# Two transposed operands made by VectorE from block-exchanged loads, in place of TensorE transposes and ScalarE copies

## The chip, the cores and the metric

The kernel runs on one core of a Trainium2 chip. The metric is the device time of one launch in microseconds (us). A launch works through 64 batch items in one program; all operands are f32. The engines are TensorE (PE; its weight loads are listed as PEld), VectorE (DVE), ScalarE (ACT), GpSimd (POOL) and SyncE (SP), which issues most DMAs.

## What is computed

For each item, x is 128 nodes by 128 features and adj a symmetric-patterned but not symmetric 128 x 128 weight matrix. Two graph layers follow each other:

```python
hi = x @ W1[:H];  hj = x @ W1[H:]
h  = relu(hi[:, None, :] + hj[None, :, :] + b1)      # all 128 x 128 pairs of nodes
y  = layernorm(h @ W2 + b2) * gamma + beta
x  = layernorm(x + einsum('ij,ijh->ih', adj, y))
# second layer
Wh = x @ W_w.T + W_b;  s = si[:, None] + sj[None, :] + a_b
e  = exp(s) * adj;     x = layernorm(x + (e / e.sum(1)) @ x)
```

Nearly all the work is the pair product: 16384 rows of 128 features per item, through the 128 x 128 matrix W2.

## The kernel before

**The slot.** One item's pair work is one slot of the program, run by every engine in its own order (`run_slots`, L152 to L161): six slots are written out, a loop with a body of eight slots turns seven times, and the last four are written out again. Within a slot there are 16 units (`u`) of eight nodes i each; a unit is two quarters (`k`) of four nodes. In slot t the engines work on three items at once: the pairs of item t (`pairs`), the weighted sum over the pairs of item t-1 (`gather`), the rest of both layers for item t-2 (`tail`), and they prepare item t+1 (`prep`). The parity p picks one of two buffers.

**The pair pipeline.** GpSimd writes the sums hi + hj of a unit into `h` (L260, a ring of four units), ScalarE applies relu in place two units ahead (L289), TensorE multiplies by `w_pair` into one of four PSUM buffers `y_ps` (L611, each product done by the helper `mm` at L535 as four column groups of 32), ScalarE copies each quarter to `y` in SBUF (L397 calls `copy`, L271), and VectorE forms the sum of squares of each row from the PSUM and the SBUF copy (L521), which frees the PSUM buffer. TensorE waits for that at L609: quarter k needs the squares of quarter k-4. The weighted sums of the item before (`weighted_sums`, L580) stand behind units 4, 6, 7, 9, 10, 12, 13 and 15 (`SUM_AT`).

**The preparation of item t+1.** SP loads x and adj two items ahead into `x_in` and `adj_in` (L185, L187), each once TensorE has read the buffer's last contents (`xT_ps_s`, `adjT_ps_s`). TensorE, ahead of unit 5, multiplies each by the identity into two quarters of the PSUM tensor `prep_ps` (`prep_transposes`, L538 to L545). ScalarE copies them to `xT` and `adjT` in unit 7 (`prep_copies`, L273, and the call at L342). TensorE, ahead of unit 9, multiplies xT by the two halves of W1 (`prep_products`, L547). VectorE moves the products to `aT` and `bT` ahead of the squares of unit 9 (`project`, L379), and GpSimd's sums read these. `adjT` is read by GpSimd at L234 and L236, as weights for the sum over the pairs.

**Other loads.** SP also loads x and adj of item t-1 a second time, as rows (`x_res`, `adj_res`, L192, L193; two semaphores, used by VectorE in unit 1 and GpSimd in unit 6 of the next slot), and stores the output (L197) when VectorE has written it in unit 14.

**The set-up** (L386 to L428 on VectorE, L554 to L573 on TensorE) builds constants and folded weights, and prepares item 0 in the same way. ScalarE's queue issues nine small loads of weights, the last of them `beta_rows`.

Each engine's order of work is written out by hand at fixed places (unit u, and on VectorE the pair e of the unit's four pairs of squares); no scheduler moves anything.

Of the kernel before, what the change touches and what calls it, by code (L numbers as in the profile page):

```python
# [33 lines left out]
def gnn_pair_kernel(nc, x, adj, W1, b1, W2, b2, gamma, beta, Ww, Wb, aw, ab, out):  # L34
# [14 lines left out]
    GROUPS, GROUP = 4, 32  # L49
# [13 lines left out]
    with ctx:  # L63
# [6 lines left out]
        def sem(name):  # L70
            return ctx.enter_context(nc.semaphore(name))
# [28 lines left out]
        xT = sb("xT", [H, S])  # L100
# [33 lines left out]
        s_two, s_zero, s_part = sem("twos_preset"), sem("wz_zeroed"), sem("parts_marked")  # L134
        x_loaded, adj_loaded, xres_loaded, stored = (
            [sem(f"{n}_{p}") for p in range(2)] for n in ("x_loaded", "adj_loaded", "xres_loaded", "out_stored"))
        xT_ps_s, adjT_ps_s, adjT_sb_s = sem("xT_in_psum"), sem("adjT_in_psum"), sem("adjT_in_sbuf")
        ab_ps_s, ab_sb_s = sem("ab_in_psum"), sem("ab_in_sbuf")
        u_ready, h_ready = sem("preact_ready"), sem("h_ready")
        y_in_psum, y_stored, q_done = sem("y_in_psum"), sem("y_stored"), sem("q_done")  # L140
# [29 lines left out]
        @block.sync  # L170
        def _(sp):

            for b in range(2):
                sp.dma_start(x_in[:, b, :], x[b]).then_inc(x_loaded[b], 16)
                sp.dma_start(adj_in[:, b, :], adj[b]).then_inc(adj_loaded[b], 16)
                if b == 0:
                    sp.dma_start(w1a[:], W1[0:H, :]).then_inc(s_w1, 16)
                    sp.dma_start(w1b[:], W1[H:2 * H, :]).then_inc(s_w1, 16)
                    sp.dma_start(b1c[:], b1.rearrange("(p o) -> p o", o=1)).then_inc(s_w1, 16)

            def slot(t, half, p, pairs, prep, gather, tail, early):
                if pairs and not (isinstance(t, int) and t + 2 >= B):

                    sp.wait_ge(xT_ps_s, t + 1)
                    sp.dma_start(x_in[:, p, :], x[bass.ds(t + 2, 1)].rearrange("o s h -> (o s) h")).then_inc(x_loaded[p], 16)  # L185
                    sp.wait_ge(adjT_ps_s, t + 1)
                    sp.dma_start(adj_in[:, p, :], adj[bass.ds(t + 2, 1)].rearrange("o s h -> (o s) h")).then_inc(adj_loaded[p], 16)  # L187
                if gather:
                    if early >= 3:

                        sp.wait_ge(x_beta_ready, t - 2)
                    sp.dma_start(x_res[:, 1 - p, :], x[bass.ds(t - 1, 1)].rearrange("o s h -> (o s) h")).then_inc(xres_loaded[1 - p], 16)  # L192
                    sp.dma_start(adj_res[:, 1 - p, :], adj[bass.ds(t - 1, 1)].rearrange("o s h -> (o s) h")).then_inc(xres_loaded[1 - p], 16)  # L193
                if tail:

                    sp.wait_ge(out_ready, t - 1)
                    sp.dma_start(out[bass.ds(t - 2, 1)].rearrange("o s h -> (o s) h"), x_out[:]).then_inc(stored[p], 16)  # L197

            run_slots(sp, slot)

            for p in range(2):
                sp.wait_ge(stored[p], 16 * (B // 2))
# [66 lines left out]
        def _(act):  # L269
            def copy(dst, src):  # L270
                return nc.scalar.activation(dst, src, ACT.Copy)  # L271

            def prep_copies(b, early):  # L273


                act.wait_ge(adjT_ps_s, b + 1)
                if early >= 1:

                    act.wait_ge(ab_ps_s, b)
                copy(xT[:], prep_ps[:, 0, :])  # L280
                if early >= 2:

                    act.wait_ge(w_ready, b - 1)
                    act.wait_ge(adjS_ready, b - 1)

            def relu(t, u):

                act.wait_ge(u_ready, t * UNITS + u + 1)
# [10 lines left out]
            act.dma_start(abc[:], ab.broadcast_to([S, 1])).then_inc(s_w, 16)  # L299
            act.dma_start(beta_rows[:], beta.rearrange("(o k) -> o k", o=1).broadcast_to([S, K])).then_inc(s_w, 16)  # L300
            nc.scalar.preload_act_table_set("natural_log_exp_and_others")
            prep_copies(0, 0)
            copy(adjT[:, 0, :], prep_ps[:, 1, :]).then_inc(adjT_sb_s, 1)
            for u in range(2):
                relu(0, u)

            def slot(t, half, p, pairs, prep, gather, tail, early):
                for u in range(UNITS):
# [27 lines left out]
                    if tail and u == 7:  # L336
# [2 lines left out]
                        nc.scalar.activation(ln1[:], mv1[:, 1:2], ACT.Ln, bias=epsc[:, 0:1]).then_inc(ln1_ready, 1)  # L339
                        act.wait_ge(ln1_ready, t - 1)  # L340
                        nc.scalar.activation(rs1[:], ln1[:], ACT.Exp, scale=-0.5).then_inc(rs1_ready, 1)  # L341
                    if prep and u == 7:  # L342
                        prep_copies(t + 1, early + 1)
                        copy(adjT[:, 1 - p, :], prep_ps[:, 1, :]).then_inc(adjT_sb_s, 1)
                    if tail and u == 9:
                        act.wait_ge(si_ready, t - 1)
                        act.wait_ge(sj_ready, t - 1)
# [28 lines left out]

        @block.vector
        def _(dve):
            def project(b, p):  # L379

                dve.wait_ge(ab_ps_s, b + 1)
                nc.vector.tensor_copy(aT[:, p, :], prep_ps[:, 2, :])
                nc.vector.tensor_scalar(bT[:, p, :], prep_ps[:, 3, :], b1c[:, 0:1], None, ALU.add).then_inc(ab_sb_s, 1)


            for p in range(2):  # L386
                nc.vector.memset(y[:, p, :, LAST:S], 2.0).then_inc(s_two, 1)
            nc.vector.memset(x1e[:], 1.0).then_inc(s_setup_dve, 1)

            dve.wait_ge(s_const, 6)  # L390
            nc.vector.reduce_sum(part[:], ident[:].rearrange("p (c s) -> p s c", s=CHUNK), axis=mybir.AxisListType.X).then_inc(s_part, 1)
# [36 lines left out]
            def slot(t, half, p, pairs, prep, gather, tail, early):  # L428

                for u, e in ((u, e) for u in range(UNITS) for e in range(2 * QPU)):  # L430
# [46 lines left out]
                    if tail and (u, e) == (7, 2):  # L477
                        nc.vector.tensor_tensor_reduce(out=s_terms[:, 0, :], in0=x1p, in1=v2row[:], scale=rs1[:, 0:1], scalar=score_c[:, 0:1],
                                                       op0=ALU.mult, op1=ALU.add, accum_out=s_ij[:, 1:2]).then_inc(sj_ready, 1)
                    if prep and (u, e) == (9, 0):  # L480
                        if early >= 1:

                            dve.wait_ge(u_ready, t * UNITS)
                        project(t + 1, 1 - p)
# [46 lines left out]
        def _(pe):  # L531
            def mm(dst, lhsT, rhs):
                for g in range(GROUPS):
                    cols = slice(g * GROUP, (g + 1) * GROUP)
                    last = nc.tensor.matmul(dst[cols], lhsT[:, cols], rhs, start=True, stop=True, tile_position=(0, g * GROUP))  # L535
                return last

            def prep_transposes(b, p, loads, later):  # L538
                pe.wait_ge(x_loaded[p], loads)
                if later:  # L540

                    pe.wait_ge(ab_sb_s, b)
                mm(prep_ps[:, 0, :], x_in[:, p, :], ident[:]).then_inc(xT_ps_s, 1)
                pe.wait_ge(adj_loaded[p], loads)
                mm(prep_ps[:, 1, :], adj_in[:, p, :], ident[:]).then_inc(adjT_ps_s, 1)  # L545

            def prep_products(b):  # L547

                pe.wait_ge(adjT_sb_s, b + 1)
                mm(prep_ps[:, 2, :], w1a[:], xT[:])  # L550
                mm(prep_ps[:, 3, :], w1b[:], xT[:]).then_inc(ab_ps_s, 1)


            pe.wait_ge(s_const, 6)  # L554
            prep_transposes(0, 0, 16, False)

            pe.wait_ge(s_w, 16 * 9)
            pe.wait_ge(s_setup_dve, 8)
# [3 lines left out]
            mm(tail_ps[:, 2, :], a2rep[:], ww[:]).then_inc(s_setup_pe, 1)  # L562
            mm(tail_ps[:, 3, 0:1], wbrep[:], a12[:]).then_inc(s_setup_pe, 1)
            pe.wait_ge(s_w1, 16 * 3)
            prep_products(0)

            pe.wait_ge(s_setup_dve, 14)
            mm(att_ps[:, 1:2], b2c_rep[:], b2c[:]).then_inc(s_setup_pe, 1)
# [15 lines left out]
            def slot(t, half, p, pairs, prep, gather, tail, early):  # L584
                for u in range(UNITS):
                    if tail and u == 3:
                        pe.wait_ge(o_stored, t - 1)
                        if gather:

                            pe.wait_ge(ln_v_ready, t)  # L590
                        mm(tail_ps[:, 0, :], o_sb[:], ident[:]).then_inc(oT_ps_s, 1)
                    if tail and u == 5:
                        pe.wait_ge(oT_sb_s, t - 1)
                        mm(tail_ps[:, 1, :], oT_sb[:], w_back[:]).then_inc(f_ps_s, 1)
                    if prep and u == 5:
                        prep_transposes(t + 1, 1 - p, nth16(half, p, 1), True)
                    if prep and u == 9:
                        prep_products(t + 1)
                    if tail and u == 11:
                        pe.wait_ge(x1s_ready, t - 1)  # L600
                        pe.wait_ge(adjS_ready, t - 1)
                        mm(att_ps[:, 0:K + 1], adjS[:, p, :], x1s[:]).then_inc(att_done, 1)
                    if pairs:

                        pe.wait_ge(h_ready, t * UNITS + u + 1)
                        for k in range(u * QPU, (u + 1) * QPU):
                            if not (early == 0 and k < YRING):

                                pe.wait_ge(q_done, t * QUARTS + k - YRING + 1)  # L609
                            for n in range(QUART):  # L610
                                last = mm(y_ps[k % YRING][:, n, :], h[:, u % HRING, (k % QPU) * QUART + n, :], w_pair[:])  # L611
                            last.then_inc(y_in_psum, 1)
                    if gather and u in SUM_AT:
                        if SUM_AT[u] == 0:

                            pe.wait_ge(w_ready, t)
                            if early >= 2:
                                pe.wait_ge(o_stored, t - 1)
                        weighted_sums(1 - p, SUM_AT[u])
# [27 lines left out]
```

## Time and profile before

| what | value |
|---|---|
| median of 3 runs | 2435.99 us (2434.59 to 2438.61) |
| the profiled execution's own time | 2439.17 us |
| its span | 2437.4 us |
| mean granted TensorE clock | 0.996 |
| busy: TensorE, weight loads, VectorE, ScalarE, GpSimd | 98%, 84%, 87%, 91%, 83% |
| DMA queue q1 | 46512 packets, 21.12 MB, 3.1% of 16 engines |

The span is from the first to the last instruction in the trace; the time of a run has some 2 us around it. Busy time of TensorE is modelled and pipelined, so that a busy engine is not one at its peak, and the durations of overlapping matmuls add up to more than the time they take. Times of single instructions in the rows below are microseconds from the start of the span unless they are marked ns. The chain of waits follows the work that ended last back from the end, at each step to what released it or to the instruction before it on the same engine.

### The profile page before, as it was taken

What the parts mean: (1) busy time and instruction counts of PE and PEld (TensorE: products, weight loads), DVE (VectorE), ACT (ScalarE), POOL (GpSimd) and SP (SyncE); (2) the same over time, 40 slices, a digit from 0 to 9 for tenths busy, and PEclk for the clock granted to TensorE, in tenths of its full rate; (3) what the DMA queues carried; (4) which work ended last, traced back from release to release, by engine and by line L of the source; (5) the groups of instructions that cost most, each with busy time, mean ns of one, the idle gap of its engine ahead of it and who ended that gap; (6) DMA issues with size and microseconds to landing.
All of it is one profiled execution on the core that took longest, in us unless ns stands there. A gap on an engine that the chain in (4) does not pass through costs nothing.

```text
span 2437.4 us, 180631 instructions
## 1 busy us (share of the span) xinstructions
PE 2377.7 (98%) x73280; PEld 2049.3 (84%) x73280; DVE 2119.3 (87%) x17881; ACT 2221.6 (91%) x3841; POOL 2021.5 (83%) x1227
## 2 busy tenths in 40 slices
PE   8999999999999999999999999999999999999997
PEld 7888888888888888888888888888788888888885
DVE  7888888888888888988888888888888988889887
ACT  7999999989999999998999989999899998999996
POOL 8888888888888888888888888888788887888884
PEclk9999999999999999999999999999999999999999
DMA  0000000000000000000000000000000000000000
GB/s 20 10 14 15 10 16 16 10 17 13 13 16 10 17 16 10 16 15 13 16 10 16 16 11 16 10 16 16 11 15 13 12 16 11 16 16 10 16 10 10
DMA packets 48682, 33.37 MB, mean 14 GB/s; under 512 B 6208, under 2 KB 47808, under 8 KB 47808
## 3 DMA queue, kind: packets, MB, share of 16 engines
q1 hardware_dynamic: 46512, 21.12, 3.1%
q8 instruction: 596, 9.76, 1.7%
q14 instruction: 278, 2.28, 0.3%
q10 hardware_dynamic: 1296, 0.20, 0.1%
HBM read 17.11 MB, written 4.19 MB: 9 GB/s over the span
## 4 chain that ended last, share of the span: by engine, by line
PE 80%; ACT 10%; issue 5%; DVE 3%; POOL 2%; ACTq 0%; DMA 0%; POOLq 0%; DVEq 0%
PE y_ps L535 59%; PE agg_ps L580 17%; ACT h L289 5%; ACT y L271 3%; PE prep_ps L535 2%; DVE squares L521 2%; POOL h L260 2%; ACT beta_part L329 1%; PE tail_ps L535 1%; ACT ln_v L318 1%; PE att_ps L535 1%; DVE q L521 0%; ACT rstd L323 0%; ACTq L370 0%; DMA beta_rows<-in_L_gnn_beta_dram 0%
## 5 line engine op out<-in xcount | busy, mean ns | idle before, releaser
L260 POOL TENSOR_TENSOR h<-bT,aT 128x1024 f32<-128x1024 f32 x1024 | 1949.6, 1918 | 360.8 <-PE y_ps L535 338.2
L535 PEld LDWEIGHTS y_ps<-w_pair,h 128*32 128x32 f32 x65536 | 1834.9, 110 | 288.2 <-issue 213.3
L521 DVE CUSTOM_DVE_ANT_0 squares<-y_ps,y 128x128 bf16<-128x128 f32 x8192 | 1853.7, 285 | 247.2 <-ACT y L271 236.6
L535 PE MATMUL y_ps<-w_pair,h 128*32 128x128 f32 x65536 | 1964.0, 273 | 38.4 <-issue 21.0
L271 ACT ACTIVATE y<-y_ps 128x508 f32<-128x508 f32 x2048 | 1153.1, 595 | 159.6 <-PE y_ps L535 153.1
L289 ACT ACTIVATE h<-h 128x1024 f32<-128x1024 f32 x1024 | 1085.0, 1060 | 23.8 <-POOL h L260 20.5
L521 DVE DVE_READ_ACCUMULATOR2_ANT q<- 128x1 f32 x8192 | 679.4, 83 | 0.2
L580 PE MATMUL agg_ps<-y,wz 128*32 128x512 f32 x4096 | 548.3, 594 | 0.0
L580 PEld LDWEIGHTS agg_ps<-y,wz 128*32 128x32 f32 x4096 | 137.1, 110 | 4.0 <-issue 3.8
L454 DVE SCALAR_TENSOR_TENSOR o_sb<-agg_ps,part,o_sb 128x128 f32<-128x128 f32 x192 | 66.5, 346 | 0.2
L234 POOL TENSOR_TENSOR wz<-adjT,rstd 128x128 f32<-128x128 f32 x64 | 33.6, 525 | 33.9 <-ACT rstd L323 33.9
L535 PEld LDWEIGHTS att_ps<-x1s,adjS 128*32 128x32 f32 x512 | 20.2, 110 | 37.6 <-issue 32.7
L513 DVE TENSOR_SCALAR x_out<-att_ps,mv,rs 128x128 f32<-128x128 f32 x64 | 26.2, 410 | 28.7 <-ACT rs L360 28.7
L535 PEld LDWEIGHTS tail_ps<-w_back,oT_sb 128*32 128x32 f32 x512 | 18.2, 111 | 37.2 <-issue 36.1
L246 POOL TENSOR_TENSOR x_beta<-beta_part,x_res 128x128 f32<-128x128 f32 x64 | 29.6, 462 | 11.2 <-ACT beta_part L329 11.2
L436 DVE TENSOR_SCALAR tail_ps<-q,bnorm 128x128 f32<-128x128 f32 x64 | 22.6, 354 | 14.5 <-issue 12.3
L472 DVE TENSOR_SCALAR x1e<-att_ps,mv,rs 128x128 f32<-128x128 f32 x64 | 26.2, 410 | 8.5 <-ACT rs L341 4.7
L535 PE MATMUL att_ps<-x1s,adjS 128*32 128x129 f32 x512 | 28.1, 275 | 3.5 <-ACT x1s L354 3.5
L535 PE MATMUL tail_ps<-ident,o_sb 128*32 128x128 f32 x512 | 26.4, 273 | 4.3 <-DVE o_sb L454 4.3
L535 PE MATMUL prep_ps<-ident,x_in 128*32 128x128 f32 x512 | 26.8, 275 | 3.1 <-DMA x_in<-in_x_dram 3.1
L329 ACT ACTIVATE beta_part<-beta_rows,adj_sum 128x128 f32<-128x128 f32 x64 | 25.5, 398 | 3.0 <-DVE adj_sum L442 3.0
L535 PE MATMUL prep_ps<-xT,w1b 128*32 128x128 f32 x512 | 28.0, 275 | 0.0
(89 smaller groups left out, 679.7 us busy)
## 6 DMA issues: line engine op xcount, KB each, us to landing
x_in<-in_x_dram SPq DMA_DIRECT2D x64, 64.0 KB, 2.5
adj_in<-in_adj_dram SPq DMA_DIRECT2D x64, 64.0 KB, 2.2
x_res<-in_x_dram SPq DMA_DIRECT2D x64, 64.0 KB, 2.0
adj_res<-in_adj_dram SPq DMA_DIRECT2D x64, 64.0 KB, 2.0
out_dram<-x_out SPq DMA_DIRECT2D x64, 64.0 KB, 1.8
w<-in_L_gnn_W_dram ACTq DMA_DIRECT2D x1, 64.0 KB, 2.3
w1a<-in_L_gnn_W_dram SPq DMA_DIRECT2D x1, 64.0 KB, 2.2
w1b<-in_L_gnn_W_dram SPq DMA_DIRECT2D x1, 64.0 KB, 2.4
```

What stands on the lines that cost most here:

```text
L234: nc.gpsimd.tensor_tensor(columns, adjT[:, 1 - p, :].rearrange("j (g c s) -> j g c s", g=GROUPS, s=CHUNK), rstd[:].rearrange("j (c s g) -> ...
L246: nc.gpsimd.tensor_tensor(x_beta[:], beta_part[:], x_res[:, p, :], ALU.add).then_inc(x_beta_ready, 1)
L260: nc.gpsimd.tensor_tensor(h[:, u % HRING].rearrange("k (r g) s -> k r g s", g=GROUPS), bT[:, p, :].unsqueeze(1).unsqueeze(1).broadcast_to( ...
L271: return nc.scalar.activation(dst, src, ACT.Copy)
L289: nc.scalar.activation(h[:, u % HRING], h[:, u % HRING], ACT.Relu).then_inc(h_ready, 1)
L329: nc.scalar.activation(beta_part[:], beta_rows[:], ACT.Identity, scale=adj_sum[:, 0:1]).then_inc(beta_part_ready, 1)
L454: nc.vector.scalar_tensor_tensor(out=o_sb[:], in0=agg_ps[:, e * K:(e + 1) * K], scalar=part[:, e:e + 1], in1=o_sb[:], op0=ALU.mult, op1=AL ...
L472: nc.vector.tensor_scalar(x1e[:, 0:K], x1p, mv1[:, 0:1], rs1[:, 0:1], ALU.subtract, ALU.mult).then_inc(x1_ready, 1)
L513: nc.vector.tensor_scalar(x_out[:], x2p, mv2[:, 0:1], rs2[:, 0:1], ALU.subtract, ALU.mult).then_inc(out_ready, 1)
L521: last = nc.vector.tensor_tensor_reduce(out=squares[:, k % YRING, n, :], in0=y_ps[k % YRING][:, n, :], in1=y[:, p, i, :], scale=1.0, scala ...
L535: last = nc.tensor.matmul(dst[cols], lhsT[:, cols], rhs, start=True, stop=True, tile_position=(0, g * GROUP))
L580: last = nc.tensor.matmul(agg_ps[g * GROUP:(g + 1) * GROUP, :], wz[:, g, chunk, :], y_chunk[:, :, g, :], start=(chunk == 0), stop=(chunk = ...
```

## The change

x and adj of an item are loaded by four DMAs each instead of one (`load_blocks`): block n of 32 partitions gets, from each block m of 32 rows, the columns of block n. So the sixteen 32 x 32 blocks arrive exchanged across the diagonal, each of them untransposed, and each contiguous run is 128 bytes. VectorE's transpose then turns each 32 x 32 block in place on its way from `x_in` to `xT` and from `adj_in` to `adjT`, ahead of the first and the third pair of squares of unit 6. The TensorE products with the identity and the two ScalarE copies go. SP's wait before the next load is for VectorE's transpose, and TensorE's products wait for xT alone. The waits that protected xT and adjT from being overwritten move from ScalarE to VectorE. In the set-up VectorE transposes item 0 before it builds its constants.

```diff
@@ SP
+            def load_blocks(dst, src, sem):
+
+                for n in range(GROUPS):
+                    rows = slice(n * GROUP, (n + 1) * GROUP)
+                    sp.dma_start(dst[rows].rearrange("r (m c) -> r m c", c=GROUP),
+                                 src[:, rows].rearrange("(m r) c -> r m c", r=GROUP)).then_inc(sem, 16)
             for b in range(2):
-                sp.dma_start(x_in[:, b, :], x[b]).then_inc(x_loaded[b], 16)
-                sp.dma_start(adj_in[:, b, :], adj[b]).then_inc(adj_loaded[b], 16)
+                load_blocks(x_in[:, b, :], x[b], x_loaded[b])
+                load_blocks(adj_in[:, b, :], adj[b], adj_loaded[b])
...
-                    sp.wait_ge(xT_ps_s, t + 1)
-                    sp.dma_start(x_in[:, p, :], x[bass.ds(t + 2, 1)].rearrange("o s h -> (o s) h")).then_inc(x_loaded[p], 16)
-                    sp.wait_ge(adjT_ps_s, t + 1)
-                    sp.dma_start(adj_in[:, p, :], adj[bass.ds(t + 2, 1)].rearrange("o s h -> (o s) h")).then_inc(adj_loaded[p], 16)
+                    sp.wait_ge(xT_sb_s, t + 1)
+                    load_blocks(x_in[:, p, :], x[bass.ds(t + 2, 1)].rearrange("o s h -> (o s) h"), x_loaded[p])
+                    sp.wait_ge(adjT_sb_s, t + 1)
+                    load_blocks(adj_in[:, p, :], adj[bass.ds(t + 2, 1)].rearrange("o s h -> (o s) h"), adj_loaded[p])
@@ ScalarE
-            def prep_copies(b, early):
-                act.wait_ge(adjT_ps_s, b + 1)
...
-                copy(xT[:], prep_ps[:, 0, :])
...
-                    if prep and u == 7:
-                        prep_copies(t + 1, early + 1)
-                        copy(adjT[:, 1 - p, :], prep_ps[:, 1, :]).then_inc(adjT_sb_s, 1)
@@ VectorE
+            def transpose_x(b, p, loads, later):
+
+                dve.wait_ge(x_loaded[p], loads)
+                if later:
+
+                    dve.wait_ge(ab_ps_s, b)
+                nc.vector.transpose(xT[:], x_in[:, p, :]).then_inc(xT_sb_s, 1)
+
+            def transpose_adj(b, p, loads, later):
+
+                dve.wait_ge(adj_loaded[p], loads)
+                if later:
+
+                    dve.wait_ge(w_ready, b - 1)
+                    dve.wait_ge(adjS_ready, b - 1)
+                nc.vector.transpose(adjT[:, p, :], adj_in[:, p, :]).then_inc(adjT_sb_s, 1)
...
             nc.vector.memset(x1e[:], 1.0).then_inc(s_setup_dve, 1)
+            transpose_x(0, 0, 16 * GROUPS, False)
+            transpose_adj(0, 0, 16 * GROUPS, False)
...
+                    if prep and (u, e) == (6, 0):
+                        transpose_x(t + 1, 1 - p, nth16(half, p, 1) * GROUPS, True)
+                    if prep and (u, e) == (6, 2):
+                        transpose_adj(t + 1, 1 - p, nth16(half, p, 1) * GROUPS, early >= 1)
@@ TensorE
-            def prep_transposes(b, p, loads, later):
-                pe.wait_ge(x_loaded[p], loads)
...
-                mm(prep_ps[:, 0, :], x_in[:, p, :], ident[:]).then_inc(xT_ps_s, 1)
-                pe.wait_ge(adj_loaded[p], loads)
-                mm(prep_ps[:, 1, :], adj_in[:, p, :], ident[:]).then_inc(adjT_ps_s, 1)
-            def prep_products(b):
-                pe.wait_ge(adjT_sb_s, b + 1)
+            def prep_products(b, later):
+                pe.wait_ge(xT_sb_s, b + 1)
+                if later:
+                    pe.wait_ge(ab_sb_s, b)
                 mm(prep_ps[:, 2, :], w1a[:], xT[:])
                 mm(prep_ps[:, 3, :], w1b[:], xT[:]).then_inc(ab_ps_s, 1)
...
-                    if prep and u == 5:
-                        prep_transposes(t + 1, 1 - p, nth16(half, p, 1), True)
                     if prep and u == 9:
-                        prep_products(t + 1)
+                        prep_products(t + 1, True)
```

## Rows read from the trace of the kernel before

**Rows 1.** The page: span, busy time by engine, and the chain by engine.
```profile
PE 2377.7 (98%) x73280; PEld 2049.3 (84%) x73280; DVE 2119.3 (87%) x17881; ACT 2221.6 (91%) x3841; POOL 2021.5 (83%) x1227
PE 80%; ACT 10%; issue 5%; DVE 3%; POOL 2%; ACTq 0%; DMA 0%; POOLq 0%; DVEq 0%
```

**Rows 2.** The chain of waits through one slot: start, length, what.
```profile
1213.20 0.04 ACT y L271
...
1219.05 1.95 PE y_ps L535 x64
...
1222.08 0.44 PE prep_ps L535 x16
1222.52 3.49 PE y_ps L535 x128
1226.01 0.86 PE agg_ps L580 x8
...
1250.21 0.04 ACT y L271
```

**Rows 3.** Groups of instructions: adj_in times identity; count, busy us, mean ns.
```profile
L535 PE MATMUL prep_ps<-ident,adj_in 128*32 128x128 f32 x512 | 26.8, 275 | 0.0
```

**Rows 4.** TensorE's timeline from the transposes (unit 5) to unit 8.
```profile
1221.90 0.40 PE L535 MATMUL prep_ps<-ident,x_in 128*32 128x128 f32 x8
...
1222.34 3.68 PE L535 MATMUL y_ps<-w_pair,h 128*32 128x128 f32 x128
...
1229.29 1.93 PE L535 MATMUL y_ps<-w_pair,h 128*32 128x128 f32 x64
```

**Rows 5.** ScalarE's timeline: relu of unit 7, the copy of xT, y copies of units 7 and 8.
```profile
1222.43 1.06 ACT L289 ACTIVATE h<-h 128x1024 f32<-128x1024 f32 x1
...
1228.14 0.28 ACT L271 ACTIVATE xT<-prep_ps 128x128 f32<-128x128 f32 x1
...
1228.47 1.09 ACT L271 ACTIVATE y<-y_ps 128x508 f32<-128x508 f32 x2
...
1231.29 0.60 ACT L271 ACTIVATE y<-y_ps 128x508 f32<-128x508 f32 x1 [0.28 <-PE y_ps L535]
```

**Rows 6.** Groups of instructions: VectorE's sum over adj_res.
```profile
L442 DVE TENSOR_REDUCE adj_sum<-adj_res 128x1 f32<-128x128 f32 x64 | 18.0, 281 | 0.0
```

**Rows 7.** The timeline of the set-up: GpSimd's first sums and VectorE's vmean.
```profile
12.41 7.52 POOL L260 TENSOR_TENSOR h<-bT,aT 128x1024 f32<-128x1024 f32 x4 [10.36 <-DVE bT L383]
12.69 1.66 DVE L415 TENSOR_SCALAR vmean<-vsum 128x2 f32<-128x2 f32 x1
```

**Rows 8.** VectorE's timeline: end of unit 5's squares, starts of units 6 and 7.
```profile
1226.04 0.08 DVE L521 DVE_READ_ACCUMULATOR2_ANT q<- 128x1 f32 x1
1226.39 0.29 DVE L521 CUSTOM_DVE_ANT_0 squares<-y_ps,y 128x128 bf16<-128x128 f32 x1 [0.26 <-ACT y L271]
...
1229.10 0.29 DVE L521 CUSTOM_DVE_ANT_0 squares<-y_ps,y 128x128 bf16<-128x128 f32 x1 [0.46 <-ACT y L271]
```

**Rows 9.** GpSimd's timeline: h of units 6 to 10.
```profile
1218.56 9.61 POOL L260 TENSOR_TENSOR h<-bT,aT 128x1024 f32<-128x1024 f32 x5
```

**Rows 10.** SP's timeline: the last two loads of a slot.
```profile
1247.44 0.38 SPq L192 DMA_DIRECT2D x_res<-in_x_dram  x1
1247.91 0.38 SPq L193 DMA_DIRECT2D adj_res<-in_adj_dram  x1
```

**Rows 11.** The page: the DMA queue of SP; a load's KB and us to landing.
```profile
q1 hardware_dynamic: 46512, 21.12, 3.1%
...
x_in<-in_x_dram SPq DMA_DIRECT2D x64, 64.0 KB, 2.5
```

**Rows 12.** The timeline of the set-up: first load, gdiag, the products of item 0.
```profile
0.75 0.39 SPq L174 DMA_DIRECT2D x_in<-in_x_dram  x1
...
7.99 0.28 DVE L395 TENSOR_SCALAR gdiag<-ident,gcol 128x128 f32<-128x128 f32 x1 [5.19 <-DMA beta_rows<-in_L_gnn_beta_dram]
...
10.56 0.66 PE L535 MATMUL prep_ps<-xT,w1a 128*32 128x128 f32 x8
```

More of the change, by code:

```diff
@@ L136, in gnn_pair_kernel @@
             [sem(f"{n}_{p}") for p in range(2)] for n in ("x_loaded", "adj_loaded", "xres_loaded", "out_stored"))
-        xT_ps_s, adjT_ps_s, adjT_sb_s = sem("xT_in_psum"), sem("adjT_in_psum"), sem("adjT_in_sbuf")
+        xT_sb_s, adjT_sb_s = sem("xT_in_sbuf"), sem("adjT_in_sbuf")
         ab_ps_s, ab_sb_s = sem("ab_in_psum"), sem("ab_in_sbuf")
@@ L271, in copy @@
                 return nc.scalar.activation(dst, src, ACT.Copy)
-            def prep_copies(b, early):
-                act.wait_ge(adjT_ps_s, b + 1)
-                if early >= 1:
-                    act.wait_ge(ab_ps_s, b)
-                copy(xT[:], prep_ps[:, 0, :])
-                if early >= 2:
-                    act.wait_ge(w_ready, b - 1)
-                    act.wait_ge(adjS_ready, b - 1)
             def relu(t, u):
@@ L301, in _ @@
             nc.scalar.preload_act_table_set("natural_log_exp_and_others")
-            prep_copies(0, 0)
-            copy(adjT[:, 0, :], prep_ps[:, 1, :]).then_inc(adjT_sb_s, 1)
             for u in range(2):
@@ L554, in _ @@
             pe.wait_ge(s_const, 6)
-            prep_transposes(0, 0, 16, False)
             pe.wait_ge(s_w, 16 * 9)
@@ L564, in _ @@
             pe.wait_ge(s_w1, 16 * 3)
-            prep_products(0)
+            prep_products(0, False)
             pe.wait_ge(s_setup_dve, 14)
```

## The prediction, as it was put on record

> **What bounds the kernel now.** First the page's busy shares and its chain of waits [rows 1]: TensorE is busy 98% of the span and carries 80% of the chain, ScalarE 10%. The busy share alone would not settle it, so I followed the chain through one slot in order of time [rows 2]. A slot is one batch item; 37.0 us of chain lie between 1213.20 and 1250.21. It has two stretches. From 1213.2 to 1219.05, the head of the slot, the chain runs through ScalarE's copies and relus and then VectorE's squares, because TensorE has nothing else between its first four units and waits for a free PSUM buffer. From 1219.05 to 1250.19, 31.1 of 37 us, the chain is TensorE and nothing else: each piece starts where the last one ends. The two transposes (16 matmul records, 0.44 us at 1222.08) lie inside that second stretch, back to back with the pair products of unit 5 behind them. The whole question is therefore whether 0.44 us taken out there stays out.
>
> **What it removes.** TensorE: eight records for x and eight for adj per item, 512 of adj over the run [rows 3] and as many of x. Their busy time and their 275 ns apiece overlap, so the price is the chain's 0.44 us per item [rows 2]. Slots 0 to 62 prepare an item (63 of them); the 64th pair of transposes is in the set-up. 63 x 0.437 = 27.5 us (0.437 is 1221.90 to 1222.34 on the matmuls' own timeline [rows 4], which is the chain's 0.44). The weight loads lie beside them and go with them. ScalarE: the copies of xT and adjT stand between 1228.14 and the next y copy at 1228.47, so they take 0.33 us of its time [rows 5]. At that place ScalarE isn't on the chain, and 3 us later, in unit 8, it waits 0.28 us for TensorE [rows 5], so I count this at nothing; it would be a gain only if ScalarE were the late one there.
>
> **What it adds on VectorE.** Two 32x32-block transposes per item, ahead of the first and third pair of squares of unit 6. No such operation stands in the trace. Nearest from below: VectorE's sum of adj_res, also 128 elements per partition of f32 from SBUF, 281 ns [rows 6]. Zero is the lower end, since they could fit into idle time. Nearest from above: vmean, 1.66 us for two elements, of which more under the rivals [rows 7]. I take 0.3 us each, next to the like-sized row, 0.6 us together if nothing overlaps. [...]
>
> Is it? The ring has four PSUM buffers, and a unit fills two, so TensorE's unit 8 needs the squares of unit 6. VectorE is through with unit 5 at 1226.04 plus the accumulator read, idles 0.26 us for ScalarE, and starts unit 6 at 1226.39; eight squares at 0.21 us end at 1228.1 [rows 8]. With 0.6 us on top, and the idle time not counted, that is 1228.7. TensorE starts unit 8 at 1229.29 [rows 4], and with the change at 1228.85, its second quarter 0.87 us later at 1229.7. The first quarter of unit 6 would be done by 1227.6, the second by 1228.7: 1.2 and 1.0 us to spare. Unit 7 has the x1 and score steps on VectorE, and an idle time of 0.46 us before its squares [rows 8] takes up most of what the transposes shift; TensorE meanwhile has the sum of unit 9 and both products ahead of what needs them. The cover is VectorE's roughly 1 us of lead over the ring; if it is gone, each further 0.1 us costs 6 us over the run.
>
> What follows the removed matmuls must also keep up. Units 5 and 6 start 0.44 us earlier, at 1221.9 instead of 1222.34 [rows 4]. GpSimd is then writing h without a pause from 1218.56 to 1228.17, five units at 1.92 us [rows 9], and is the engine I looked at longest: those are h of units 6 to 10, and unit 7 isn't needed before 1226.2, when its h has been ready since 1222.4 and its relu since 1223.5 [rows 5]. No loss there. At the end of the slot all engines wait for TensorE again, so the next head starts in the same state, and its stall (16 units at 1.745, 8 sums at 0.86 and 7 small products at 0.22 are 36.3 us of work [rows 2], so 0.7 us per slot) stays as it was. I count no gain and no loss for it.
>
> **What moves on the queues.** The loads become eight DMAs of 16 KB in place of two of 64 KB, in 128-byte runs. SP issues its DMAs in one burst ahead of each slot, 0.47 us apart [rows 10]; six more are 2.8 us of SP. Behind them stand x_res and adj_res, not needed before unit 1 of the next slot, over 35 us later, and behind those the wait for the output, which comes 30 us later. x and adj themselves are asked for about two units before a slot and read in unit 6 of the slot after it. The new waits on SP (xT and adjT in SBUF) were met in unit 6 of the slot before. The hardware queue q1 holds 46512 packets and 3.1% of 16 engines' time [rows 11]: 1209 us of engine time, 26 ns a packet. The change adds 64 x 2 x 384 = 49152 packets; at the same 26 ns, the upper end, that is 80 us more for each of 16 engines over the run, 3.3% of the span. Lower end: nothing, since the bytes stay the same. Hidden either way, with 50 us between the issue and the use. The added wait on VectorE for loads that landed long ago holds up nothing.
>
> **The start.** VectorE now waits for x and adj before the constants part, centre and basis. SP issues every 0.47 us from 0.75, so the eighth load goes out at 4.0 and lands by 6.5 (2.5 us to landing [rows 11]); two transposes and 0.7 us of constants end near 7.9. The next step, gdiag, starts at 7.99 when beta_rows has landed [rows 12]. w1a, w1b and b1c go out six issues later, b1c at about 5.4, and land at 8.2; TensorE wants them at 10.56 [rows 12]. So 0 to 1 us, and I take 0.5.
>
> **The sum.** 27.5 - 0.5 = 27.0 us off. The profiled execution took 2439.2 us with a span of 2437.4, which makes 2412.2 for it; the median of the three runs is 2436.0, 3.2 below, and from it the forecast is **2409 us**, 1.1% faster. A measurement of this kernel can tell about 0.2%, 5 us, from no change.
>
> **Rival 1: the shared memory port (slower).** In the set-up vmean, a VectorE operation on two elements from SBUF to SBUF, starts at 12.69, 0.28 us into GpSimd's first h, and ends at 14.35, just as that h (1.9 us) does [rows 7]. It was shut out by GpSimd. None of VectorE's operations in the steady part suffers this, but nearly all have an operand in PSUM; the transposes have not. If they are shut out likewise, each waits up to 1.92 us, since GpSimd runs without a gap just there [rows 9], and 0.96 in the mean. Against 1.0 us of lead plus 0.44 gained, it decides from 1.44 us of waiting per slot on: two mean waits (1.92) make 0.5 us per slot lost, 30 us, 2467; two full ones 2.4 us, 2587. Against it: adj_sum reads and writes SBUF alone too, also with GpSimd working, and takes 281 ns in the mean of 64 [rows 6]. [...] Chance 0.12.
>
> **Rival 2: the gain is partly given back.** Units 5 and 6 run without a sum between them, and ScalarE goes from y copy to relu almost without a gap after the head. If TensorE, 0.44 us earlier, meets a ring that ScalarE or VectorE hasn't emptied, or six more DMAs in SP's burst delay something behind them, half goes: 2422 (2416 to 2430). For it: the head does end in just such a wait. Against: 0.7 us or more of margin by the rows above. Chance 0.16. If all of it goes, the time stays at 2436: 0.05.
>
> **Rival 3: more than the matmuls.** Taking 0.33 us from ScalarE and a dependence from the middle could also shorten the head; 0.1 us per slot makes 2402. Nothing in the chain speaks for it. Chance 0.05.
>
> **Chances and range.** The forecast 0.62 (2403 to 2416), rival 1 0.12, rival 2 0.16 and its full form 0.05, rival 3 0.05. From 2401 to 2430 the range holds the forecast, rival 3's nearer half and rival 2. Faster by over 0.2%: 0.82; within 0.2%: 0.06; slower: 0.12.
>
> **What would show it.** The chain after: y_ps of unit 5 right behind tail_ps with no prep_ps piece, one prep_ps piece of 0.44 us left per slot, and 36.6 us from one slot's ln_v to the next. Transposes of about 0.3 us with GpSimd's h running over them show rival 1 wrong; durations of 1 to 2 us there, and TensorE's wait for q in units 8 and 9, show it right. VectorE's busy time should rise by 30 us or so, ScalarE's fall by 21 to 35. Slots that are still 37.0 us long with a longer head would mean rival 2.

## The result, and the profile after

The changed kernel takes 2402.9 us (median of four runs, 2401.0 to 2405.5) against 2435.5 of the kernel before: 32.5 us less, ratio 0.986 with a 95% interval of 0.985 to 0.987. The forecast was 2409, its range 2401 to 2430. The profiled execution took 2405.5 us with a span of 2403.7, 33.7 below the span before. One execution among the later runs (narrow products with the long body) took 8712.7 us for no reason that the record shows, and it is left out of that run's median.

The page after: busy time and instructions, the DMA queue of SP, the chain by engine and a load's KB and time to landing.

```profile
PE 2345.1 (98%) x72256; PEld 2016.5 (84%) x72256; DVE 2125.4 (88%) x18009; ACT 2195.9 (91%) x3713; POOL 2018.9 (84%) x1227
...
q1 hardware_dynamic: 101808, 21.15, 4.2%
...
PE 82%; ACT 9%; issue 4%; DVE 3%; ACTq 0%; POOL 0%; DMA 0%; DVEq 0%
...
x_in<-in_x_dram SPq DMA_DIRECT2D x256, 16.0 KB, 1.9
```

TensorE has 1024 matmuls fewer and is busy 32.6 us less, about what the kernel gained [rows 1]. Its share of the chain rose from 80% to 82%: it is still what bounds the kernel. Now the chain through one slot, to be laid beside [rows 2]; columns are start, length, what.

```profile
1197.65 0.04 ACT y L278
...
1203.50 1.95 PE y_ps L547 x64
1205.45 0.86 PE agg_ps L585 x8
1206.31 0.22 PE tail_ps L547 x8
1206.53 3.49 PE y_ps L547 x128
1210.02 0.86 PE agg_ps L585 x8
...
1215.23 0.44 PE prep_ps L547 x16
...
1234.22 0.04 ACT y L278
```

The 3.49 us piece of units 5 and 6 stands directly behind the small tail product; the 0.44 us piece that lay between them is gone, and the one of the W1 products is left. From one "ACT y" row to the other the slot is 36.57 us. The head of the slot, from 1197.65 to 1203.50, is 5.85 us long, as before (1213.20 to 1219.05). So the 0.43 us stayed out, and the head didn't take it back.

What VectorE got for it, in groups (count, busy us, mean ns of one) and on the timeline of unit 6:

```profile
L374 DVE STREAM_TRANSPOSE xT<-x_in 128x128 f32<-128x128 f32 x64 | 19.7, 307 | 2.8 <-DMA x_in<-in_x_dram 2.8
L383 DVE STREAM_TRANSPOSE adjT<-adj_in 128x128 f32<-128x128 f32 x64 | 19.6, 306 | 1.6 <-DMA adj_in<-in_adj_dram 1.6
```
```profile
1210.41 0.30 DVE L374 STREAM_TRANSPOSE xT<-x_in 128x128 f32<-128x128 f32 x1
1210.64 0.25 DVE L533 CUSTOM_DVE_ANT_0 squares<-y_ps,y 128x128 bf16<-128x128 f32 x1
...
1211.46 0.30 DVE L383 STREAM_TRANSPOSE adjT<-adj_in 128x128 f32<-128x128 f32 x1
```
```profile
1203.02 9.41 POOL L267 TENSOR_TENSOR h<-bT,aT 128x1024 f32<-128x1024 f32 x5
```

A transpose takes 0.31 us (0.30 in this slot), but the squares behind it start 0.23 us after its start. The third fence is GpSimd's timeline: both transposes run inside its 9.4 us without a pause, and neither waits.

The start didn't get longer. VectorE's timeline of the set-up:

```profile
6.19 0.31 DVE L383 STREAM_TRANSPOSE adjT<-adj_in 128x128 f32<-128x128 f32 x1 [1.65 <-DMA adj_in<-in_adj_dram]
...
6.80 0.28 DVE L401 TENSOR_TENSOR basis<-house,ident 128x128 f32<-128x128 f32 x1
7.88 0.29 DVE L403 TENSOR_SCALAR gdiag<-ident,gcol 128x128 f32<-128x128 f32 x1 [0.80 <-DMA beta_rows<-in_L_gnn_beta_dram]
```

The constants are ready by 7.1 and gdiag still waits 0.80 us for beta_rows; it starts 0.11 us earlier than before [rows 12].

**Where 33 us come from.** The time between two starts of ln_v (ScalarE, once a slot) gives the length of every slot. I took the commonest length as the regular slot and added up by how much the others are longer. Six slots in each trace are 2.9 to 4.6 us longer; they are the ones where the loop turns back (seven passes of eight slots, so six turns).

| trace | regular slot | six slots with a turn, excess | the other slots, excess |
|---|---|---|---|
| before | 37.00 | 21.1 | 12.9 |
| after | 36.57 | 23.2 | 3.8 |

Regular slots give 0.43 x 63 = 27.1 us, the term of the forecast (27.5). Strictly it is 26.7, since the first of the 63 gave nothing back: the first ln_v starts at 52.90 us before and at 52.89 after. The rest is in irregular slots, 34.0 us together before and 27.0 after. The turns are no shorter after than before; the difference is in the other slots. Most of those before are not scattered: the second slot after a turn takes 37.74 us or more in five passes, and the fourth 37.3 to 38.0 in all six. In the second, TensorE pauses in unit 6 for nothing that the timeline can name:

```profile
586.09 1.25 PE L535 MATMUL y_ps<-w_pair,h 128*32 128x128 f32 x34 [0.40 <-issue]
```

One execution each is thin ground for that part, since it differs from one execution to the next; the experiments take it up.

### The profile page after: what moved, and what is told of

The parts are those of the page before. It is cut to its first block, busy times and chain, and to the rows that moved or that the text cites. A ratio compares the mean times of both kernels' runs of the same rounds, so it can differ in the third digit from the quotient of the medians.

```text
span 2403.7 us, 179414 instructions
## 1 busy us (share of the span) xinstructions
PE 2345.1 (98%) x72256; PEld 2016.5 (84%) x72256; DVE 2125.4 (88%) x18009; ACT 2195.9 (91%) x3713; POOL 2018.9 (84%) x1227
## 3 DMA queue, kind: packets, MB, share of 16 engines
q1 hardware_dynamic: 101808, 21.15, 4.2%
## 4 chain that ended last, share of the span: by engine, by line
PE 82%; ACT 9%; issue 4%; DVE 3%; ACTq 0%; POOL 0%; DMA 0%; DVEq 0%
PE y_ps L547 62%; PE agg_ps L585 18%; ACT h L283 5%; ACT y L278 3%; DVE squares L533 2%; PE prep_ps L547 1%; ACT beta_part L321 1%; PE tail_ps L547 1%; ACT ln_v L310 1%; PE att_ps L547 1%; DVE q L533 1%; POOL h L267 0%; ACTq L359 0%; ACT rstd L315 0%; DMA beta_rows<-in_L_gnn_beta_dram 0%
## 5 line engine op out<-in xcount | busy, mean ns | idle before, releaser
L547 PEld LDWEIGHTS att_ps<-x1s,adjS 128*32 128x32 f32 x512 | 19.1, 110 | 38.5 <-issue 33.9
L253 POOL TENSOR_TENSOR x_beta<-beta_part,x_res 128x128 f32<-128x128 f32 x64 | 29.6, 463 | 11.2 <-ACT beta_part L321 11.2
L547 PE MATMUL tail_ps<-w_back,oT_sb 128*32 128x128 f32 x512 | 28.1, 273 | 0.4 <-ACT oT_sb L278 0.4
L547 PE MATMUL prep_ps<-xT,w1a 128*32 128x128 f32 x512 | 28.3, 275 | 0.0
```

What stands on the lines that cost most here:

```text
L253: nc.gpsimd.tensor_tensor(x_beta[:], beta_part[:], x_res[:, p, :], ALU.add).then_inc(x_beta_ready, 1)
```

## The experiments

The theory: all of the gain is TensorE's time, because the chain runs through TensorE where the transposes stood, and VectorE (also beside a busy GpSimd), ScalarE and the queues have room for the rest. The rivals: ScalarE's copies count too; VectorE's transposes are hidden only by luck, with no lead left; the loads cost something. And a question: whose are the 5 us beyond the regular slots? In what follows each time is to be compared with 2402.9 and, by its ratio, with the kernel before on the same chip.

### The TensorE products put back

```diff
+                    if prep and u == 5:
+                        mm(prep_ps[:, 0, :], ident[:], ident[:])
+                        mm(prep_ps[:, 1, :], ident[:], ident[:])
                     if prep and u == 9:
                         prep_products(t + 1, True)
```

> The changed kernel with two products of the identity with itself put back on TensorE ahead of unit 5, in the place and of the size of the old transposes; nothing reads them, the output stays whole. Theory A (all of the gain is TensorE's): the slot goes from 36.57 back to 37.00 us and the time to 2430 to 2436, 0.44 us x 63 = 27.5 up, and a further 5 to 6 if the irregular slots of 37.3 to 38.0 us of the kernel before come back too. Theory B (part of the gain is ScalarE's copies): it stays at least 5 us below the kernel before, at 2430 or less, with regular slots of 37.00.

Measured: 2435.3 us, ratio 1.0007 (0.9997 to 1.0017) to the kernel before. The regular slot is 37.00 us again. Both transposes on VectorE, the loads in blocks and the missing copies on ScalarE are all in this kernel, and it takes the time of the kernel before: these three together are worth nothing that the interval can tell (0.7 us of gain to 4.1 of loss), and the gain is TensorE's. Theory B is out.

### Narrow products in their place

```diff
+                    if prep and u == 5:
+                        mm(prep_ps[:, 0, 0:4], ident[:], ident[:, 0:4])
+                        mm(prep_ps[:, 1, 0:4], ident[:], ident[:, 0:4])
```

> As the run before, but the products put back are 4 columns wide instead of 128: the same 16 instructions and weight loads on TensorE's queue, little of the time. If the irregular slots come from the number of instructions that TensorE has to take in, they come back here (5 to 6 us) and the regular slot grows by the cost of narrow products alone; by their timing alone the irregular slots stay away. If a product costs by its weight load and not by its columns, the regular slot is at 37.0 again; if it costs by its columns, at 36.6 to 36.75 (2403 to 2415 us).

Measured: 2425.1 us, ratio 0.9954 (0.9938 to 0.9969). Its chain:

```profile
1253.54 0.20 PE tail_ps L547 x6
1253.75 0.12 PE prep_ps L547 x15
1253.86 3.52 PE y_ps L547 x128
```

The sixteen instructions take 0.12 us in place of 0.44, and the regular slot is 36.69. So a product's price in the slot is mostly its columns. Yet the kernel is 22.1 us slower than the changed one, of which 0.12 x 63 = 7.6 are regular slots. The other 14 are irregular ones: the six turns are 33.4 us too long in sum (23.2 in the changed kernel), the other slots 6.3 (3.8). So the time missed what I had expected (2403 to 2415, or 5 to 6 us for irregular slots), though in the direction of "by the number of instructions".

### The ScalarE copies put back

```diff
+                    if prep and u == 7:
+                        copy(spare[:, 0, :], ident[:])
+                        copy(spare[:, 1, :], ident[:])
```

> The changed kernel with two 128x128 copies put back on ScalarE in unit 7 (from a constant to a spare tensor, so from SBUF rather than PSUM); the output stays whole. Theory A: ScalarE has idle time there, so 2403 within 5 us and slots of 36.57. Theory B: ScalarE's 0.33 to 0.5 us count and up to 0.4 us a slot come back, or the irregular slots do: 2408 to 2425.

Measured: 2402.9 us, ratio 0.9869 (0.9853 to 0.9886), regular slot 36.57. ScalarE is busy 13 us more and nothing else moves. Taking the copies away was free and worth nothing.

### A plain copy in place of the transpose

```diff
-                nc.vector.transpose(xT[:], x_in[:, p, :]).then_inc(xT_sb_s, 1)
+                nc.vector.tensor_copy(xT[:], x_in[:, p, :]).then_inc(xT_sb_s, 1)
...
-                nc.vector.transpose(adjT[:, p, :], adj_in[:, p, :]).then_inc(adjT_sb_s, 1)
+                nc.vector.tensor_copy(adjT[:, p, :], adj_in[:, p, :]).then_inc(adjT_sb_s, 1)
```

> Each block transpose on VectorE is replaced by a plain copy of the same tile between the same tensors, so x and adj come out with wrong contents and the time alone is read. This is the rival of the shared port, made to happen: if a plain f32 copy from SBUF to SBUF is shut out while GpSimd works and the transpose is not, the copies take 0.2 to 2.0 us each, some 1 us in the mean, against 0.31 for the transposes, TensorE waits for q in units 8 and 9, and the time is 2403 to 2470 by how much of VectorE's lead is left; by the prediction's bound nothing is lost below 1.0 us more per slot and 6 us per 0.1 us above it. If a copy isn't shut out either, they take 0.22 us and the time is 2403.

Measured: 2419.1 us, ratio 0.9935 (0.9918 to 0.9952). Groups of instructions (count, busy, mean ns), then VectorE's timeline in an early and a middle slot:

```profile
L383 DVE COPY adjT<-adj_in 128x128 f32<-128x128 f32 x64 | 73.4, 1148 | 1.6 <-DMA adj_in<-in_adj_dram 1.6
L374 DVE COPY xT<-x_in 128x128 f32<-128x128 f32 x64 | 29.3, 458 | 2.9 <-DMA x_in<-in_x_dram 2.9
```
```profile
100.39 2.00 DVE L374 COPY xT<-x_in 128x128 f32<-128x128 f32 x1
...
103.15 1.68 DVE L383 COPY adjT<-adj_in 128x128 f32<-128x128 f32 x1
...
1221.87 1.11 DVE L383 COPY adjT<-adj_in 128x128 f32<-128x128 f32 x1
```

GpSimd's timeline of the same middle slot, and TensorE's of the early one:

```profile
1213.47 9.42 POOL L267 TENSOR_TENSOR h<-bT,aT 128x1024 f32<-128x1024 f32 x5
```
```profile
105.73 1.08 PE L547 MATMUL y_ps<-w_pair,h 128*32 128x128 f32 x32 [1.26 <-DVE q L533]
```

GpSimd does shut VectorE out here, only not for a transpose. The same tile between the same tensors takes 0.22 to 0.23 us as a copy when it gets in, but the copy of adjT ends at 1222.98, just behind the end of GpSimd's five sums at 1222.89, and in the early slot both copies wait, 3.2 us together. The other slots agree: each of the 126 copies behind the set-up ends 0.08 to 0.11 us after the end of one of GpSimd's operations, and none lies within one. Of the changed kernel's 128 transposes 67 lie within one, and all take 0.30 to 0.31 us. In the mean adjT takes 1.15 us as a copy against 0.31 as a transpose. Why the one is shut out and the other is not, no run shows.

This run also measures VectorE's lead. In the regular slots the 0.9 us that adjT waits cost nothing: they are 36.57 us long. In the slots with 3.2 us of waiting TensorE stands 1.26 us for q in unit 8, and the slot is 38.55, 1.98 longer; so 1.2 to 1.3 us were absorbed.

### More transposes than needed

```diff
                 if later:
+                    for _ in range(3):
+                        nc.vector.transpose(spare[:, _, :], x_in[:, p, :])
```

The second run has 8 in place of 3. (The `if later:` around the loop is new as well and adds nothing else.)

> The changed kernel with three more block transposes of x ahead of the one in unit 6, into a spare tensor; the output stays whole. They cost VectorE 0.2 to 0.23 us each, 0.6 to 0.7 us a slot. By the prediction's lead of 1.0 us nothing is lost: 2403 within 5 us, slots of 36.57. If VectorE has no lead left after the change, each 0.1 us is paid with 6 us: 2440 to 2450.

> The same with eight more, 1.7 to 1.85 us of VectorE per slot. By the prediction's lead of 1.0 us some 0.7 to 0.85 us a slot are lost and the slot is 37.3 to 37.4: 2447 to 2457 us. By the run with plain copies, whose slots with 3.3 us of added VectorE time grew by 1.98, the lead is 1.3 us and the slot 37.0: 2428 to 2440 us.

Measured: 2404.7 us (ratio 0.9868, 0.9852 to 0.9885) with a regular slot of 36.57 for three, and 2432.1 us (0.9978, 0.9969 to 0.9988) with one of 37.03 for eight. The chain of the second runs through VectorE up to unit 8:

```profile
1225.15 1.07 DVE spare L377 x6
...
1226.72 0.19 DVE xT L378
1226.92 0.17 DVE squares L537
...
1231.19 0.20 DVE squares L537
...
1231.46 1.08 PE y_ps L551 x32
```

Nine transposes take from 1225.15 to 1226.92, 0.197 us each, so eight add 1.6 us; 0.46 of it reaches the slot. So the lead that the change leaves is 1.1 us, where the prediction had 1.0 and the copies gave 1.2 to 1.3; the time lies in the band that I had put down by the copies (2428 to 2440), below the one by the prediction. The two transposes of the change take 2 x 0.23 us ahead of that lead, and three more fit into it.

### The loads alone

```diff
-                    sp.dma_start(x_in[:, p, :], x[bass.ds(t + 2, 1)].rearrange("o s h -> (o s) h")).then_inc(x_loaded[p], 16)
+                    load_blocks(x_in[:, p, :], x[bass.ds(t + 2, 1)].rearrange("o s h -> (o s) h"), x_loaded[p])
```

and the same for adj and in the set-up, in the kernel before.

> The kernel before with only the loads of x and adj changed to the eight block-exchanged DMAs, still transposed whole by TensorE, so that the contents are wrong and the time alone is read. Theory (the loads are hidden): the time of the kernel before within 5 us. Rival (128-byte runs or SP's longer burst cost something, and the change would have gained more without them): 2440 or more.

Measured: 2438.3 us, ratio 1.0004 (0.9995 to 1.0014); the regular slot is 37.00. The loads cost nothing, with q1 at the same 101808 packets and 4.2% as in the changed kernel.

### A lighter head

```diff
-    POOL_WEIGHTS_UNIT, POOL_RESIDUAL_UNIT = 5, 6
+    POOL_WEIGHTS_UNIT, POOL_RESIDUAL_UNIT = 5, 7
...
-                    if tail and u == 2:
+                    if tail and u == 3:
                         act.wait_ge(adj_sum_ready, t - 1)
```

> An attempt at a better version: in the changed kernel ScalarE's beta_part moves from unit 2 to unit 3, behind the y copies of unit 2 that the head of the slot waits for, and GpSimd's sum with x_res from unit 6 to unit 7. The output stays whole. If the head is ScalarE's work in order, its 0.29 us leave the chain: slots of 36.3 and 2384 us. If VectorE or GpSimd is right behind, it is 2395 to 2403; if the later x_beta reaches VectorE's unit 5 too late, it is slower than 2403.

Measured: 2394.5 us, ratio 0.9826 (0.9809 to 0.9842). The head of its chain:

```profile
1226.42 0.02 issue
1226.44 0.07 DVE squares L533
...
1228.52 0.30 DVE o_sb L458
...
1230.42 0.20 DVE squares L533
1230.81 0.28 DVE squares L533
1231.10 0.20 DVE squares L533
1231.37 1.08 PE y_ps L547 x32
```

The regular slot is 36.28, as forecast, but the time fell by 8.5 us and not by 19: the other slots' excess is 11.9 us in this trace against 3.8. Where the chain of the head left ScalarE one microsecond ahead of TensorE's next piece (1202.51 to 1203.50 in the changed kernel), it now runs through almost five microseconds of VectorE's o_sb steps and squares, so VectorE is what is next there, and slots are irregular more often. Why they are is not settled.

### Fewer turns of the loop

```diff
-    PEEL, LOOP_END, BODY = 6, B - 2, 8
+    PEEL, LOOP_END, BODY = 6, B - 2, 28
```

The first of these runs is the changed kernel with this line, the second adds the lighter head, the third the narrow products, and the last the full products.

> The changed kernel with a loop body of 28 slots in place of 8, so that the loop turns back once instead of six times; the same instructions are executed in the same order. In the changed kernel's trace the six slots with a turn are 23.2 us longer in sum than regular ones, 3.9 each, TensorE waiting for nothing but its own next instruction at their start. If the turn itself costs that, five go: 2384 us. If it is the rate at which instructions come in, whatever the turns, it stays at 2403, or the pauses move elsewhere.

> Both attempts at a better version together: beta_part one unit later (measured 2394) and the body of 28 slots. If the two are independent and the turns cost what they seem to: 2394 - 19 = 2375 us. If the turns' cost only moves: 2394.

> The kernel with 16 narrow products more on TensorE per slot (measured 2425, 22 us above the changed kernel, of which its regular slots explain 0.12 x 63 = 7.6) with the body of 28 slots. If the rest, some 14 us, sat in the turns, where its six long slots are 33.4 us longer in sum against 23.2, this is only 8 to 10 us above the run with the body of 28 alone. If it is the number of instructions as such, it is again 20 us or more above it.

> The full-width products put back on TensorE (measured 2435.3 with the body of 8 slots, 32.3 above the changed kernel) with the body of 28 slots. The regular slots explain 0.43 x 63 = 27.1. If the other 5 us sit in the turns of the loop, this is 27 us above the body-of-28 run's 2386.6: 2413 to 2415. If they are spread over the slots or belong to the products themselves, it is 32 above: 2418 to 2420. Both differences carry some 3 us of scatter.

TensorE's timeline at a turn of the changed kernel, before the change of this line:

```profile
820.34 1.04 PE L585 MATMUL agg_ps<-y,wz 128*32 128x512 f32 x8
824.09 6.88 PE L547 MATMUL y_ps<-w_pair,h 128*32 128x128 f32 x192 [2.72 <-issue]
```

TensorE stands 2.72 us and waits for nothing that the profile shows; this is between the last weighted sum of one pass and the first unit of the next. Measured, with the sums over the slots of each trace:

| kernel | body | us | ratio to before (interval) | regular slot | all excess (turns) |
|---|---|---|---|---|---|
| changed | 8 | 2402.9 | 0.9861 (0.9849 to 0.9874) | 36.57 | 27.0 (23.2) |
| changed | 28 | 2386.6 | 0.9792 (0.9771 to 0.9813) | 36.57 | 9.0 (3.9) |
| + lighter head | 28 | 2374.0 | 0.9744 (0.9725 to 0.9762) | 36.28 | 14.9 (3.9) |
| + narrow products | 8 | 2425.1 | 0.9954 (0.9938 to 0.9969) | 36.69 | 39.7 (33.4) |
| + narrow products | 28 | 2397.8 | 0.9847 (0.9822 to 0.9872) | 36.69 | 11.5 (3.7) |
| + full products | 8 | 2435.3 | 1.0007 (0.9997 to 1.0017) | 37.00 | 30.1 (25.0) |
| + full products | 28 | 2413.3 | 0.9893 (0.9876 to 0.9909) | 37.00 | 10.9 (4.6) |

With one turn in place of six, 16 us go. The excess of the turns goes with their number, 3.7 to 4.6 us for the one that is left. Sixteen narrow products cost 22.1 us with the short body and 11.2 with the long one; the full products 32.3 and 26.7, where the regular slots alone give 27.1. The last of these differences is between two chips. By the ratios, which allow for the chip, the full products cost 36 us (32 to 39) and 25 us (18 to 31). The part beyond the regular slots is there with six turns and within the scatter of zero with one, so the surplus over the forecast goes with the short body, by a margin that is just clear of the intervals. The four runs had been expected at 2384, 2375, 8 to 10 us above the first, and 2413 to 2415; they took 2386.6, 2374.0, 11.2 above it, and 2413.3.

The traces don't place it in the turning slots themselves, though. Their excess is 21.1 us before, 25.0 with the products back, and anywhere from 19.1 to 25.8 in five kernels without them (the changed one, the ScalarE copies, three and eight more transposes, the lighter head). Only the narrow products' 33.4 stand out, and since that is above the full products' 25.0 with the same number of instructions, the number isn't all of it.

What TensorE waits for at a turn is in no chain, but the DMA records tell something of it. The profile's page lists a queue of "instruction" packets. Here it is before, then after, then from 821.0 to 822.6 of the trace after, just ahead of the pause shown above (packets, MB, share):

```profile
q8 instruction: 596, 9.76, 1.7%
```
```profile
q8 instruction: 588, 9.63, 1.7%
```
```profile
q8 instruction: 1, 0.02, 5.6%
```

A packet is 16 KB. With the short body there are 588 of them in the changed kernel and 587 or 588 in every run that adds work to ScalarE or VectorE alone, but 595 when the products are back, full or narrow. By these counts I take this queue to bring TensorE its instructions. The packet of the last line lands at 822.50, and TensorE goes on at 824.09, 1.6 us later. The same holds in all 14 traces: of the pauses of TensorE put down to "issue", the 62 longer than 2 us end 1.6 to 1.9 us after such a packet has landed, and the 73 from 0.18 to 1 us, the one at 586.09 among them, 1.2 to 1.7 us after. A moment taken at random lies that far behind a packet in 12 to 18% of cases. And a turn's pause is longer when its packet took longer: 1.0 to 1.6 us of packet and 2.6 to 2.8 of pause in the changed kernel, 1.5 to 2.3 and 2.9 to 3.8 with the narrow products. So TensorE seems to wait for its own instructions, at the turns and at some other places of a pass. This is read from times that agree; no run changed the packets alone. How much of the surplus is fewer or shorter waits of this kind is not measured.

The best kernel of these is the one with the lighter head and the long body: 2374.0 us, 29 below the changed kernel.

## Why the prediction was right

**TensorE's 0.44 us per slot.** Right: 37.00 to 36.57 for the regular slot, forecast 36.6. The step that carried it, that a piece inside an unbroken TensorE stretch of the chain is paid in full, is shown by putting the products back (1.0007). That 2402.9 is inside the range is in part luck: it lies 2 us from its lower end, at the edge of the forecast's own band (2403 to 2416), and next to rival 3's 2402, whose mechanism did not happen.

**ScalarE's copies at nothing.** Right, by putting them back. ScalarE's busy time fell by 25.7 us, forecast 21 to 35.

**VectorE's transposes.** 0.31 us each, forecast 0.3; their step on the queue is 0.2 to 0.23. The lead was put at 1.0 us and measured at 1.1 to 1.3. Wrong was only the busy time, forecast to rise by 30 us: it rose by 6, from 2119.3 to 2125.4, though the transposes add 128 x 0.23 = 29. The squares' records are 0.29 us long, and where nothing holds them up the next ones start 0.21 us after, so that squares add 0.21 us of busy time when the next ones follow at once and 0.29 when they don't. VectorE's waits for ScalarE's y copies fell from 624 to 513 in number: each wait that goes takes back some 0.08 us of busy time, 9 us in all. The rest of the difference I haven't traced. It had no bearing on the sum.

**The queues.** q1 has 55296 packets more, not 49152. The 6144 above are 384 more DMAs times 16, which I had left out (what the 16 packets are, no run shows). Its share rose from 3.1% to 4.2%, about 26 us per engine where the upper end was 80: a packet now takes 16 ns in the mean and not 26. The loads alone change nothing (1.0004).

**The start.** Put at 0.5 us, it cost none.

**The surplus.** Forecast 27, measured 32.5. The interval of the ratio makes that 31 to 37, so the surplus is clear of the noise. The term that was too small is the removed products' own: it was priced from a regular slot alone. The trace before already had six slots of 39.9 us and more among 37s, and eleven of 37.3 to 38.0 at fixed places of the pass, and I had not priced what 16 instructions fewer do there. The runs show that the surplus goes with the short body (the products cost 36 us with six turns and 25 with one); why it does is open. Rival 3 had its eye on the right side and named the wrong place; the head of the regular slot kept its 5.85 us.

**Rival 1,** that GpSimd shuts VectorE out, fell for the transpose and stood for a copy, but at 2419 us and not at the 2467 that two mean waits gave: in a regular slot the copy of xT met only the end of a sum and took 0.23 us, and the 0.9 us that the copy of adjT waited stayed within the lead. That a memory port is shared, as its title has it, no run shows; the runs show when the copies ended. **Rival 2** fell: the regular slot gave back nothing of its 0.43 us.

## What to carry to other kernels

Price a removed instruction at its piece in the chain, and check that the stretch it lies in is one engine's without a break; then measure the lead of the engine that takes the work over, which here was 1.1 us beyond the 0.46 that the work needed. Before giving VectorE an SBUF-to-SBUF operation beside a busy GpSimd, ask whether it is a kind that is shut out: copy 1.15 us, transpose 0.31. And list the length of every pass of a loop, not of a typical one: the slots with a turn were 3.9 us longer in the mean, and a longer body took 16 us off a kernel that was taken for bound by its matmuls.

## What the hardware showed that I had not expected

At each turn of a loop with some 9000 TensorE matmul and weight-load pairs in its body (72256 in 64 slots, times eight) the slot was 3 to 5 us longer in the kernels before and after, with TensorE waiting for no other engine; in all traces it went on 1.6 to 1.9 us after a 16 KB packet of instructions had landed. Sixteen products of 4 columns took 0.12 us where those of 128 took 0.44, and yet cost 22 us over the kernel with the short body, 14 of them in irregular slots, and 11 with the long one. And 128-byte runs in place of 512-byte ones took the mean time of a packet on q1 from 26 to 16 ns, so four times as many runs for the same bytes of x and adj raised the queue's share by 1.1 points only.
